# Gathering attention: who multiplies the third context row by its weights

## The reference

```python
indices = clip([p, p + 1, p + 2], 0, l - 1)      # three context rows for each token
win_states = advisor_states[indices]             # gathered
sj = (hidden @ Wqj.T) . (win_states @ Wkj.T) / sqrt(h)   # 3 scores; rules on them by the row's id
aj = softmax(sj);  cj = sum_w aj[w] * (win_states @ Wvj.T)[w]
si, ai, ci           # the same with Wqi, Wki, Wvi, without the rules
context = w[0] * cj + w[1] * ci
out = context @ Wout.T * gain                    # added to the stream
```

## Time and profile before

| what | value |
|---|---|
| time, median of 3 runs | 1950.97 us (1949.88 to 1953.06) |
| profiled execution, time | 1950.5 us |
| its span in the trace | 1948.4 us |
| PE busy | 1738.0 us (89%) |
| ACT busy | 1348.9 us (69%) |
| DVE busy | 1038.9 us (53%) |
| POOL busy | 241.1 us (12%) |
| chain that ended last, by engine | PE 50%, ACT 20%, DVE 8%, issue 12% |

### The profile page before, as it was taken

The page is one execution under the profiler, slowest core; times in us unless marked ns, Lnnn a source line. Parts: engine busy times, 40 slices in busy tenths (PEclk is TensorE's granted clock), DMA queues, the critical chain, the costliest instruction groups (busy, mean ns, idle before and its releaser), DMA issues.

```text
span 1948.4 us, 47109 instructions
## 1 busy us (share of the span) xinstructions
PE 1738.0 (89%) x19832; PEld 1121.8 (58%) x19832; DVE 1038.9 (53%) x2670; ACT 1348.9 (69%) x1589; POOL 241.1 (12%) x160
## 2 busy tenths in 40 slices
PE   0556999999999989998999999999998899999998
PEld 0345999999998844454544554545444355555554
DVE  3996222222224345555555555555446877777774
ACT  0344444444443379999999999999998577767665
POOL 6355000000000110000000000000000121211222
PEclk9867999999999989999999999999999999999999
DMA  8001000000000233333333333333350000000000
GB/s 283 1 1 46 1 1 1 1 1 1 1 1 1 63 78 83 82 82 82 81 76 81 75 81 73 80 75 79 65 128 4 1 6 6 7 1 6 6 6 11
DMA packets 36213, 85.68 MB, mean 44 GB/s; under 512 B 10649, under 2 KB 23330, under 8 KB 35618
## 3 DMA queue, kind: packets, MB, share of 16 engines
q1 hardware_dynamic: 33954, 76.30, 16.6%
q0 software_dynamic: 2048, 6.36, 1.1%
HBM read 30.43 MB, written 2.10 MB: 17 GB/s over the span
## 4 chain that ended last, share of the span: by engine, by line
PE 50%; ACT 20%; issue 12%; DVE 8%; DVEq 1%; ACTq 0%; POOL 0%; POOLq 0%
ACT C_probs L1903 18%; PE C_ps_s L692 14%; PE C_ps_s L679 10%; PE C_ps_s L1143 6%; PE C_ps_s L1152 6%; PE C_ps_o L1800 3%; DVE C_den_t L2067 3%; PE C_ps_s L1785 2%; PE C_ps_o L1168 2%; PE C_ps_p L1133 2%; PE C_ps_p L1734 1%; DVE D_gated L1371 1%; PE C_ps_p L1741 1%; DVEq L2030 1%; PE C_ps_s L697 1%
## 5 line engine op out<-in xcount | busy, mean ns | idle before, releaser
L1903 ACT ACTIVATE C_probs<-C_ps_s 128x1024 f32<-128x1024 f32 x832 | 773.6, 1067 | 54.4 <-PE C_ps_s L1785 53.8
L1800 PE MATMUL C_ps_o<-C_probs,C_values 128*16 128x256 f32 x6656 | 442.2, 383 | 10.5 <-DVE C_o_t L2063 9.8
L1231 ACT ACTIVATE D_hidden<-C_ps_s,D_b_up 128x1024 f32<-128x1024 f32 x256 | 275.4, 1113 | 134.3 <-PE C_ps_s L1143 133.9
L753 ACT ACTIVATE B_hidden<-C_ps_s,B_b_up 128x512 f32<-128x512 f32 x288 | 191.9, 688 | 197.3 <-PE C_ps_s L679 196.7
L692 PE MATMUL C_ps_s<-B_w_down,B_hidden 128*128 128x128 f32 x2304 | 277.5, 277 | 0.0
L692 PEld LDWEIGHTS C_ps_s<-B_w_down,B_hidden 128*128 128x128 f32 x2304 | 271.4, 193 | 10.4 <-ACT B_hidden L753 1.2
L1785 PE MATMUL C_ps_s<-C_queries,C_keys 32*128 32x256 f32 x3328 | 212.4, 329 | 37.3 <-ACT C_probs L1903 36.4
L1800 PEld LDWEIGHTS C_ps_o<-C_probs,C_values 128*16 128x16 f32 x6656 | 154.5, 96 | 150.2 <-ACT C_probs L1903 12.4
L1785 PEld LDWEIGHTS C_ps_s<-C_queries,C_keys 32*128 32x128 f32 x3328 | 127.3, 184 | 168.2 <-ACT C_probs L1903 120.1
L852 DVE SCALAR_TENSOR_TENSOR B_acc<-C_ps_s,B_gate,B_acc 128x128 f32<-128x128 f32 x224 | 63.1, 344 | 273.5 <-PE C_ps_s L692 273.5
L1143 PE MATMUL C_ps_s<-D_up_in,D_w_up_r 128*128 128x512 f32 x512 | 185.8, 444 | 3.7 <-issue 1.9
(11 more groups left out here) (275 smaller groups left out, 1956.4 us busy)
## 6 DMA issues: line engine op xcount, KB each, us to landing
C_keys<-C_k_hi SPq DMA_DIRECT2D x128, 200.1 KB, 4.2
C_ctx_t<-ctx_t_dram SPq DMA_DIRECT2D x16, 800.5 KB, 4.4
C_keys<-C_k_lo SPq DMA_DIRECT2D x64, 200.1 KB, 4.1
C_queries<-C_q_hi SPq DMA_DIRECT2D x128, 32.0 KB, 2.3
B_w_up<-L_ffn_w_up_dram SPq DMA_DIRECT2D x1, 2304.0 KB
B_w_down<-L_ffn_w_down_dram SPq DMA_DIRECT2D x1, 2304.0 KB
C_queries<-C_q_lo SPq DMA_DIRECT2D x64, 32.0 KB, 2.3
C_queries<-C_blank SPq DMA_DIRECT2D x16, 128.0 KB, 2.6
```

The costliest lines, as they stand in the source:

```text
L753: nc.scalar.activation(hidden[:, e % HB, c, :], ps_h[c][:], ACT.Gelu, bias=b_up[:, u:u + 1]).then_inc(s_hid, 1)
L1231: nc.scalar.activation(hidden[:, u % RING, :, :], ps_u[u % 2][:], ACT.Gelu, bias=b_up[:, u % PAIRS:u % PAIRS + 1]).then_inc(s_hid, 1)
L1800: m = T.matmul(ps_o[32 * j:32 * j + 2 * DK, g % 2, :], values[:, parity, kt, g * HG + j, :], probs[:, slot(parity, 2 * step + j // 2), j % ...
L1903: nc.scalar.activation(probs[:, slot(parity, n)], ps_s[bank(parity, n)][:], ACT.Exp, scale=SCORE_SCALE1).then_inc(s_exp, 1)
```

## The change

GpSimd's multiply is taken out. ScalarE forms the products of the third row too, with the same instruction as the first two, into the same place (z[:, k % 2, 2]). GpSimd keeps its three adds and waits for all three products. Block 7 is made as before; VectorE's wait there has another number, since ScalarE counts 24 instead of 16 for each block ahead of it.

```diff
-                    tiles, third = slice(k * BT, (k + 1) * BT), (WIN - 1) * D
                     parts = z[:, k % 2]
-                    wait(pool, s_mix, 1 + sum(k >= first for first, _ in PARTS[1:]))
-                    chain.mark(nc.gpsimd.tensor_tensor(
-                        parts[:, 2], window[:, tiles, third:third + D].unsqueeze(2).to_broadcast([P, BT, 2, D]),
-                        mix[:, WIN - 1, :, tiles].rearrange("p q t -> p t q").unsqueeze(3).to_broadcast([P, BT, 2, D]),
-                        ALU.mult))
-                    pool.wait_ge(s_first, 4 * BT * (k + 1))
+                    pool.wait_ge(s_first, 2 * WIN * BT * (k + 1))
                     chain.step(nc.gpsimd.tensor_tensor(parts[:, 0], parts[:, 0], parts[:, 1], ALU.add))
...
                 def mixes(k):
-                    dve.wait_ge(s_first, 4 * BT * k + 2 * BT)
+                    dve.wait_ge(s_first, 2 * WIN * BT * k + 2 * BT)
...
                     wait(act, s_ztr, 2 * (k - 1))
-                    for w in range(1 if k in BY_DVE else 2):
+                    for w in range(1 if k in BY_DVE else WIN):
                         for i in range(BT):
                             t = k * BT + i
                             for q in range(2):
```

## The result

The changed kernel takes 1957.98 us in the median of 7 runs (1954.74 to 1966.95) against 1950.97 us (1948.97 to 1953.06). The ratio is 1.0038, 95% interval 1.0024 to 1.0052: slower by 0.38%, 7.0 us between the medians. The forecast was 1957.4 us.

A forecast was written before the change was run, and what follows sets the result against it. VectorE was taken to set the pace, partly stalled by GpSimd; after the change ScalarE's order costs. Third weights +4.1 us and tail +2.3 sum to +6.4, 1957.4 us; range 1952.5 to 1962.

The forecast's parts named there:

- add of block 0: VectorE's add to the stream after block 0's output product: at 95.8 to 97.5 us, against 96.84 before.
- second weights: VectorE's weights after the adds of blocks 0 and 1: ready at 118.9 to 119.0 us, +1.0.
- third weighing: VectorE's weighing after block 3's add: starts at 140.2 us instead of 133.57, +6.6; lasts 8.0 plus 4.3 us.
- third weights: Result of VectorE's weighing after block 3's add: ready at 152.5 us against 148.36, +4.1.
- What VectorE wins it gives back as waiting: Blocks 0 and 1: the 6.9 us VectorE has won at 85.0 become a wait for ScalarE.
- The small logic operations are held up by GpSimd: L400 to L432 beside GpSimd's adds of block 5: between 0 and 4.3 us lost, 4.3 taken.
- The tail: Block 6's products, ahead of block 5's zt copies and block 7's products, are 2.33 us longer, all on the path.
- The clock: TensorE's output products take 2.05 us at the high clock, 3.79 at the low; blocks 1 and 3 taken as low.
- mild loss: Rival: high clock for blocks 1 and 3 (+2.9 us), or logic operations pass GpSimd (+2.1); 1953 to 1954, chance 0.22.
- Low clock throughout: Rival: output products of blocks 0 and 7, with their transposes, are slow too; +10.4 us, 1961, chance 0.10.
- VectorE didn't stay the bound: Rival: ScalarE's copies come in time, 12.4 us on four normalisations less 2.33 in the tail; -10 us, 1941, chance 0.05.
- The full load of ScalarE: Rival: the added products of all seven blocks lie on the path, 7 x 2.33 = +16.3 us, 1967, chance 0.03.

The follow-up runs named there:

- the four corners: First-layer stretch with GpSimd's multiply at 16 and 24 ScalarE products a block: 89.72 and 97.74 us; without the multiply: 80.55 and 96.38 us.
- kernel 4: Changed kernel with block 6's multiply back on GpSimd and 16 products there: tail from 21.53 to 19.59 us, first-layer stretch 93.64 us, ratio to before 1.0019.
- Kernel 8: Changed kernel with 12, 24 and 12 idle transposes on TensorE in blocks 0, 1 and 3: first-layer stretch 92.25 us, ratio to before 1.0008.
- kernel 1: Changed kernel without the third row's products in blocks 0 to 6, so neither multiply nor replacement: first-layer stretch 80.55 us, ratio to before 0.9960.
- kernels 7: Kernel before with only block 1's multiply moved from GpSimd to ScalarE: first-layer stretch 87.10 us, ratio to before 0.9975.
- 5: Kernel before with only blocks 1 and 5 moved from GpSimd's multiply to ScalarE's products: first-layer stretch 84.28 us, ratio to before 0.9967.
- 5 again: Second run of the kernel before with only blocks 1 and 5 moved to ScalarE: first-layer stretch 82.94 us, ratio to before 0.9955.

## Why the prediction was right

The mechanism, the places and the size held. Step by step, in the time of the changed kernel's first profile:

| step | predicted | measured |
|---|---|---|
| normalisations of blocks 4, 5 and 7, four instructions | 1.1 us | 1.11 |
| add of block 0 | 95.8 to 97.5 | 97.03 |
| add of block 1 | 109.1 | 109.88 |
| second weights (normalisation of block 7) | 119.0 | 119.68 |
| third weighing starts | 140.2 | 140.73 |
| third weights (end of their last operation) | 152.5 | 152.79 |
| tail longer by | 2.33 | 2.32 |
| next layer's start later by | 6.4 | 6.8 |

*What VectorE wins it gives back as waiting:* shown by the waits, and by the four corners, in which the removal is worth 9.2 us with 16 products and 1.4 with 24.

*The small logic operations are held up by GpSimd:* I took the high bound, 4.3 us. The third weighing takes 12.1 us (140.73 to 152.79) against the estimate of 8.0 without GpSimd: 4.1 us lost. The prediction's nearest row was the cast. The trace of before had a nearer one, three two-input operations at the front of the same weighing, beside GpSimd's instructions, which take 0.44 us together in the changed kernel without them:

```profile
134.58 4.34 DVE L381 TENSOR_TENSOR A_picked<-A_where,A_found 128x48 f32<-128x48 f32 x3
```

*The tail:* shown by kernel 4.

*The clock* was the weakest part. The sum had the low clock in for the output products of blocks 1 and 3 and walked on from block 0 at the high one. Block 0 ran mostly at the low one, 3.41 us, 1.4 more, and the second weights came 0.7 us late. The walk of the blocks behind them was some 0.4 us too long, so the third weights came only 0.3 late: two small errors of opposite sign, and part of the closeness of 6.4 to 6.8 is luck. Kernel 8 shows the clock to be the largest single item, 4.1 of 6.7 us. What is left without it, 2.5 us (1.0008, not clear of 1), is near the +2.9 us that the prediction gave its mild loss for the high clock in blocks 1 and 3. "Low clock throughout" was half true: block 0's product was slow, block 7's took 2.05 us.

*The rivals.* VectorE didn't stay the bound; its price without the products and their tail (12.4 us on the normalisations) was too high. In kernel 1 the four give back 9.3, since the adds of block 0 still hold up the normalisation of block 5, 4.24 instead of 1.11 us. The third weighing, 12.2 us there instead of 14.8, gives back 2.6 more, and new waits of 1.02 and 1.10 us for output products take some of it: 9.2 in all were measured. The full load of ScalarE (16.3 us) didn't appear against before, but 15.8 us did against kernel 1: once GpSimd's stall is gone, the same number of products costs twice what it costs beside the stall, the clock's share included.

*A wrong reading:* that each multiply of GpSimd ends before ScalarE's products do. In the trace of before this holds for blocks 0, 2, 3 and 6. The multiplies of blocks 1, 4 and 5 end 1.7, 1.7 and 2.7 us after the products, and GpSimd's own adds start behind them. The sum did not use it.

*Not foreseen:* waits for the queries' products came before two halves only, 5.3 us in all, not before all of blocks 4 to 7. And the 3.3 us behind the first layer, beyond the sum in that profile, are scatter; by the stretches alone the change costs 6.7 to 6.9 us, by the ratios 7.2 to 7.4.

## What to carry to other kernels

Before moving work off an engine that "only helps", see what it holds up without being waited for (here GpSimd's multiply beside VectorE's normalisations), and then where in its order the receiving engine will do it: ScalarE stood idle for 48% of the stretch, and this bought little, because most of the added products were queued ahead of a copy that TensorE and then VectorE needed. Such a move pays block by block, where the added products have cover and the removed instruction stood in the way: two blocks of seven gained 5 to 7 us, all seven lost 7. And a wait put in front of TensorE costs more than its length, as the matmuls behind it may find the low clock.

## What the hardware showed that I had not expected

Small VectorE operations of 8 elements a lane are held up beside a GpSimd add as large ones are: one scalar_tensor_tensor of 128x8 at 142.62 took 2.21 us, against 0.17, and ended at 144.83, as GpSimd's add did at 144.80. The prediction had this only as a bound. The Trainium skill, SBUF — State Buffer, section "Who interferes with whom", says that of VectorE and GpSimd the one that issues first has the shared ports for its whole instruction, and that issue order, not shape, decides who is blocked; the trace agrees. So these two engines don't meet only at semaphores, as the start of this document has it.

Twelve to 24 idle transposes ahead of a late matmul group gave back 1.3 to 1.7 us each time (3.41, 3.78 and 3.78 us became 2.05, 2.51 and 2.05), more than I had expected of work that computes nothing.

And the same program doesn't find the same clock in every execution: 16 output matmuls of block 1 took 3.68, 2.74 and 2.05 us in kernels 7, 5 and 5 again. A gain of 1 or 2 us, read from one profile each, can be that and nothing else.
